# The order of one attention body: first scores before the router's transpose, the keys' projection before the fourth maxima product, the router's logits one place later

## The chip, the cores and the metric

One core of a Trainium2 chip runs the whole program. The metric is the device time in microseconds (us) of one execution. The kernel before was run three times: 950.31 us in the median, 949.5 the lowest and 953.55 the highest. The engines are TensorE (PE), VectorE (DVE), ScalarE (ACT), GpSimd (POOL) and SyncE (SP), which issues DMAs. Each runs its own list of instructions in order, and they meet at semaphores.

## The reference

Two layers work on x of shape (8, 256, 256). Each layer adds gated cross attention (16 heads of 16) and then a gated mixture of experts (8 experts, two per token) to x.

```python
x = x + tanh(g_xattn[0]) * attention(layernorm(x), ctx, L0 weights)
x = x + tanh(g_ffn[0])   * moe0(layernorm(x))      # logits = xn @ gate_w, top 2, softmax of the two, gelu experts
x = x + tanh(g_xattn[1]) * attention(layernorm(x), ctx, L1 weights)
x = x + tanh(g_ffn[1])   * moe1(layernorm(x))      # logits = xn @ router_w.T + b, softmax, top 2, capacity 256, relu experts
# attention: q, k, v = projections with bias; softmax(q k^T / 4) v per head; output projection with bias
```

The change is within the attention, in both layers. The attention phase also computes the router's layer norm and logits for the mixture that follows it.

## The kernel before, in words

`attention_phase` is called once for each layer. It works batch by batch (8 batches of 256 tokens) as a software pipeline written out by hand: each engine has a loop over "bodies" b = -3 to 9, and one body holds pieces of up to five batches. For the batch b+3 it makes the normalised input and turns it; for b+2 it projects queries, keys and values; for b+1 it takes the row maxima of the scores; for b it computes scores, exponentials and the weighted values; for b-1 it finishes the second half of the heads, the output projection and the residual; for b-2 it turns the router's rows and multiplies them with the gate's weights. Bodies 2 to 5 hold all of these (bodies 0 and 1 have no router work, bodies 6 to 9 have no projections of queries, keys and values any more). The order of the instructions in each engine is the order of the calls in its loop: TensorE L719 to L789, ScalarE L402 to L427, VectorE L529 to L565.

The pieces that the change touches, with their names in the code:

- `head_scores(b, i)`, i = 0 to 7 (L638): two products of 32 rows with 512 columns each, into the two banks `ps_max`. VectorE's `take_maxima(b, i)` (L463) reduces them (two reductions), and `head_scores(b, i+1)` waits until that is done, since the banks are used again.
- `scores(b, c)`, c = 0 to 3 (L658): 16 products of 17 rows (16 of the head and one with the row's maximum) into `ps_st`, the one buffer of four banks. `scores(b, 0)` waits for the DMAs that lay queries, keys and maxima into their slots; each of the four waits for the exponential before it, which frees `ps_st`. ScalarE's `probabilities(b, c)` (L386) is that exponential over 128x2048 elements.
- `weigh_values(b, c)` (L672): 16 products of the probabilities with the values, into `ps_head`; `turn_heads` (L685) turns the heads after ScalarE has copied them out (`heads`, L392), and VectorE's `normalise` (L473) divides by the sums.
- The bank `ps_lin` is a single buffer that eight pieces use in turn. In a full body of the kernel before, the turns are: queries, the router's transpose, the router's logits, keys, values, the transpose of the attention's output, the transpose of the normalised input, and the output projection. Each writes only after the one before it has been copied out by ScalarE or VectorE. ScalarE's `router_inputs` (L370) copies the router's transpose (semaphore `rt_ready`); VectorE's `router_logits` (L500) copies the logits (`lg_done`); ScalarE's `keys` copies the projected keys and adds their bias (`k_evac`); ScalarE's `separate_keys` (L347) then makes two masked copies of the keys for a later body's `head_scores`.

For batches whose keys are projected in the same body as a router turn (keys of batch 4 to 7, bodies 2 to 5), the projection waits for that body's router logits to have been copied:

```python
            def keys(b):
                pe.wait_ge(ctx_split, b + 1)
                wait(pe, lg_done, b - 3)
```

`fill` issues dummy transposes, only in bodies below 0 and above 6, where TensorE has less to do.

SP issues the DMAs of a body in a fixed order (L239 to L248): queries to slots, keys to slots, the context of batch b+4, the maxima of batch b+1 to slots, and the router's rows. The change leaves SP's and POOL's lists as they are.

Of the kernel before, what the change touches and what calls it, by code (L numbers as in the profile page):

```python
# [13 lines left out]
B, S, D = 8, 256, 256  # L14
# [68 lines left out]
def attention_phase(nc, layer, shared, dram, load_x):  # L83
# [4 lines left out]
    with ExitStack() as ctx:  # L88
# [249 lines left out]
        @block.scalar  # L338
        def _(act):
            def project(b, ps_sem, evac, ld, bias, compact):  # L340
                act.wait_ge(ps_sem, b + 1)
                wait(act, ld[(b - 2) % 3], SLOTTED * ((b - 2) // 3 + 1))
                for c in range(KC):
                    act.activation(compact[b % 2][:, c, :], ps_lin[:, c * S:(c + 1) * S], ACT.Identity,
                                   bias=bias[:, c:c + 1]).then_inc(evac, 1)

            def separate_keys(b):  # L347
                act.wait_ge(k_evac, 2 * b + 2)
                wait(act, s_ps, 8 * (b - 1))
                for j in range(2):  # L350
                    act.activation(k_r[b % 2][:, :, j, :], k_c[b % 2][:, :, :], ACT.Copy,
                                   scale=shared["odd_head"][:, j:j + 1]).then_inc(k_round, 1)

            def queries(b):
                wait(act, q_round, b - 1)
                if b == 0:
                    act.wait_ge(wq_ld, 32)
                project(b, q_ps, q_evac, q_ld, bq, q_c)

            def keys(b):  # L360
                if b == 0:
                    act.wait_ge(wk_ld, 32)
                project(b, k_ps, k_evac, k_ld, bk, k_c)

            def inputs(b):
                act.wait_ge(xt_ps, b + 1)
                wait(act, q_ps, b)
                act.activation(xn_t[0][:, :, :], ps_lin[:, :].rearrange("p (k s) -> p k s", k=KC), ACT.Copy).then_inc(xt_hi, 1)

            def router_inputs(b):  # L370
                act.wait_ge(rt_ps, b + 1)
                wait(act, lg_ps, b)
                act.activation(xr_t[:, :, :], ps_lin[:, :].rearrange("p (k s) -> p k s", k=KC), ACT.Copy).then_inc(rt_ready, 1)

            def maxima(b):
                act.wait_ge(mt_ps, b + 1)
                wait(act, m_ld, 16 * CH * b)
                act.activation(m_t[:, :], ps_max[0][0:H, :, :].rearrange("p q s -> p (q s)")[:, 0:S], ACT.Copy,
                               scale=-1.0).then_inc(mt_ready, 1)

            def outputs(b):
                act.wait_ge(ot_ps, b + 1)
                wait(act, out_ps, b)
                act.activation(o_t[0][:, :, :], ps_lin[:, :].rearrange("p (k s) -> p k s", k=KC), ACT.Copy).then_inc(ot_hi, 1)

            def probabilities(b, c):  # L386
                n = b * CH + c
                act.wait_ge(st_ps, n + 1)
                wait(act, pv_ps, n - 1)
                act.activation(prob[n % 2][:, :, :, :], ps_st[:, :, :, :], ACT.Exp, scale=HD ** -0.5).then_inc(prob_ready, 1)  # L390

            def heads(b, u):  # L392
                n = b * OCT + u
                act.wait_ge(pv_ps, 2 * n + 2)
                wait(act, turned, n - 1)
                act.activation(head_t[n % 2][:, :, :], ps_head[:, :].rearrange("p (c s) -> p c s", c=2), ACT.Copy).then_inc(head_out, 1)

            for n, w, ld in (("wq", wq, wq_ld), ("wk", wk, wk_ld), ("wv", wv, wv_ld), ("wo", wo, wo_ld)):
                act.wait_ge(ld, 32)
                act.activation(w[0][:, :, :], w_raw[n][:, :, :], ACT.Copy).then_inc(w_hi, 1)  # L400

            for b in BODIES:  # L402
                if is_batch(b + 2):
                    queries(b + 2)
                if is_batch(b - 1):
                    heads(b - 1, 1)
                if is_batch(b - 2):
                    router_inputs(b - 2)
                if is_batch(b):
                    probabilities(b, 0)  # L410
                if is_batch(b + 2):
                    keys(b + 2)
                    separate_keys(b + 2)
                if is_batch(b):
                    probabilities(b, 1)
                if is_batch(b - 1):
                    outputs(b - 1)
                if is_batch(b):
                    heads(b, 0)
                if is_batch(b + 3):  # L420
                    inputs(b + 3)
                if is_batch(b):
                    probabilities(b, 2)
                if is_batch(b + 1):
                    maxima(b + 1)
                if is_batch(b):
                    probabilities(b, 3)  # L427

        @block.vector
        def _(dve):  # L430
# [98 lines left out]
            for b in BODIES:  # L529
                if is_batch(b + 3):  # L530
                    if not load_x:
                        combine(b + 3)
                    moments(b + 3)
                if b == -3:
                    weights_first()
                if is_batch(b + 1):
                    take_maxima(b + 1, 0)
                    take_maxima(b + 1, 1)
                    take_maxima(b + 1, 2)
                if is_batch(b - 2):  # L540
                    router_logits(b - 2)
                if is_batch(b + 1):
                    take_maxima(b + 1, 3)
                if is_batch(b - 1):
                    normalise(b - 1, 1)
                if is_batch(b + 1):
                    take_maxima(b + 1, 4)
                if is_batch(b + 2):
                    values(b + 2)
                if is_batch(b + 1):  # L550
                    take_maxima(b + 1, 5)
                if is_batch(b - 1):
                    outputs_low(b - 1)
                if is_batch(b + 1):
                    take_maxima(b + 1, 6)
                if is_batch(b + 3):
                    inputs_low(b + 3)
                if is_batch(b + 1):
                    take_maxima(b + 1, 7)
                if is_batch(b - 1):  # L560
                    residual(b - 1)
                    router_moments(b - 1)
                if is_batch(b):
                    normalise(b, 0)
# [3 lines left out]
        def _(pe):  # L568
# [21 lines left out]
            def router_logits(b):  # L590
                if b == 0:
                    pe.wait_ge(gate_ld, 16 + 16 * layer)
                wait(pe, rt_ready, b + 1)
                for q in range(QT):
                    for k in range(KC):
                        ins = pe.matmul(ps_lin[:, q * E:(q + 1) * E], xr_t[:, k, q * P:(q + 1) * P], gate_w[:, k, :],
# [26 lines left out]
            def keys(b):  # L623
                if b == 0:
                    pe.wait_ge(w_split, 2)
                pe.wait_ge(ctx_split, b + 1)
                wait(pe, lg_done, b - 3)
                if b < 4:
                    wait(pe, q_evac, 2 * (b + 1))
                heads_project(wk, ctx_t[b % 2], k_ps)  # L630

            def values(b):
                if b == 0:
                    pe.wait_ge(w_split, 3)
                wait(pe, k_evac, 2 * (b + 1))
                token_major(ctx_t[b % 2], wv, v_ps)

            def head_scores(b, i):  # L638
# [80 lines left out]
            for b in BODIES:  # L719
# [10 lines left out]
                    head_scores(b + 1, 1)  # L730
                if is_batch(b - 1):
                    weigh_values(b - 1, 3)
                if is_batch(b - 2):
                    router_turn(b - 2)
                if is_batch(b + 1):
                    fill(b, True, 6 if b == -1 else 0)
                    head_scores(b + 1, 2)
                if is_batch(b):
                    scores(b, 0)
                if is_batch(b - 2):  # L740
                    router_logits(b - 2)
                if is_batch(b - 1):
                    turn_heads(b - 1, 1)
                    fill(b, False, 8)
                if is_batch(b + 1):
                    fill(b, True, 6 if b == -1 else 0)
                    head_scores(b + 1, 3)
                if is_batch(b + 2):
                    keys(b + 2)
                    fill(b, True, 6 if b == -2 else 0)  # L750
                if is_batch(b + 1):
                    fill(b, True, 6 if b == -1 else 0)
                    head_scores(b + 1, 4)
                if is_batch(b):
                    fill(b, False, 8)
                    scores(b, 1)
                if is_batch(b + 2):
                    values(b + 2)
                if is_batch(b + 1):
                    fill(b, True, 6 if b == -1 else 0)  # L760
                    head_scores(b + 1, 5)
                if is_batch(b):
                    weigh_values(b, 0)
                if is_batch(b - 1):
                    o_transpose(b - 1)
                    fill(b, False, 8)
# [758 lines left out]
```

## Time and profile before

| what | value |
|---|---|
| median of three runs | 950.31 us |
| the profiled execution's own time | 947.15 us |
| its span on the core | 945.4 us |
| mean granted TensorE clock, as a share of full speed | 0.901 |
| PE busy | 788.8 us (83%) |
| DVE busy | 640.2 us (68%) |
| ACT busy | 450.0 us (48%) |
| POOL busy | 361.9 us (38%) |

The span comes from one profiled execution. A busy share is an average over phases with different limits: the attention of layer 0 runs from about 14 to 232 us, its experts from about 260 to 550, the attention of layer 1 from about 563 to 800, and its experts to the end. Matmul ends are modelled, so a matmul's row is best read by its start and the start of what follows it.

### The profile page before, as it was taken

The numbers are of one execution on the slowest core, as the hardware profiler recorded it, in microseconds if no ns is written. First come the engines' busy times: TensorE is split into PE (matmuls) and PEld (weight loads), VectorE is DVE, ScalarE is ACT, GpSimd is POOL, SyncE is SP. The second block draws the span as 40 slices with busy tenths as digits, with TensorE's granted clock in tenths as the row PEclk, the third lists the DMA queues.
The fourth block names the chain that finished last, engine by engine and source line by source line (L and its number), as shares of the span: only waits on it lengthen the run. The fifth ranks groups of instructions, "written<-read, shape, count | busy, mean of one in ns | idle before, by whom it ended". The sixth has DMA issues, their size and how long they took to land. (4 is left out here: it accounts for less than half of the span.)

```text
span 945.4 us, 17859 instructions
## 1 busy us (share of the span) xinstructions
PE 788.8 (83%) x7040; PEld 670.8 (71%) x7040; DVE 640.2 (68%) x1172; ACT 450.0 (48%) x648; POOL 361.9 (38%) x390
## 2 busy tenths in 40 slices
PE   5799999896359999999999837899999896329995
PEld 4666777564359999999999836666667555328995
DVE  3667777632758999999999434676677632768883
ACT  2256666542056666666665211364556552315541
POOL 8434552112153333333331088656432112331653
PEclk8979999999569999999999967797999889558998
DMA  5211111000366777667774043222211000545732
GB/s 170 65 37 39 50 49 38 24 24 23 140 203 230 245 241 249 238 235 237 240 246 160 34 135 87 59 72 56 55 47 36 24 24 13 191 155 203 222 81 34
DMA packets 49814, 111.39 MB, mean 118 GB/s; under 512 B 11970, under 2 KB 35011, under 8 KB 42051
## 3 DMA queue, kind: packets, MB, share of 16 engines
q0 software_dynamic: 13056, 65.30, 21.7%
q1 hardware_dynamic: 36674, 44.95, 15.3%
q8 instruction: 56, 0.92, 0.4%
q14 instruction: 28, 0.22, 0.1%
HBM read 87.08 MB, written 14.49 MB: 107 GB/s over the span
## 5 line engine op out<-in xcount | busy, mean ns | idle before, releaser
L471 DVE TENSOR_REDUCE mx_a<-ps_max_a 128x2 f32<-128x512 f32 x256 | 164.4, 684 | 65.2 <-PE ps_max_a L647 63.0
L390 ACT ACTIVATE prob_a<-ps_st_a 128x2048 f32<-128x2048 f32 x64 | 120.0, 1875 | 56.9 <-PE ps_st_a L668 56.9
L71 PE MATMUL ps_h_e<-xe_t_e,w_e 128*128 128x256 f32 x480 | 140.2, 292 | 8.2 <-DVE xe_t_e L1380 8.2
L73 PE MATMUL ps_h_e<-xe_t_e,w_e 128*128 128x256 f32 x480 | 137.3, 286 | 0.0
L72 PE MATMUL ps_h_e<-xe_t_e,w_e 128*128 128x256 f32 x480 | 137.1, 286 | 0.0
L71 PE MATMUL ps_y_e<-w_e,h_e 128*128 128x256 f32 x480 | 133.2, 277 | 0.0
L72 PE MATMUL ps_y_e<-w_e,h_e 128*128 128x256 f32 x480 | 133.0, 277 | 0.0
L73 PE MATMUL ps_y_e<-w_e,h_e 128*128 128x256 f32 x480 | 133.0, 277 | 0.0
L1310 ACT ACTIVATE hid_e<-ps_h_e,b_e 128x256 f32<-128x256 f32 x184 | 78.4, 490 | 94.4 <-PE ps_h_e L73 94.4
L864 POOL DMA_INDIRECT w_raw_w<-L_w,block_row x46 | 43.6, 947 | 164.8 <-DVE b_e L1352 81.1
L71 PEld LDWEIGHTS ps_h_e<-xe_t_e,w_e 128*128 128x128 f32 x480 | 94.8, 198 | 9.4 <-DVE xe_t_e L1380 9.4
L72 PEld LDWEIGHTS ps_h_e<-xe_t_e,w_e 128*128 128x128 f32 x480 | 94.3, 196 | 0.0
L73 PEld LDWEIGHTS ps_h_e<-xe_t_e,w_e 128*128 128x128 f32 x480 | 93.9, 196 | 0.0
L71 PEld LDWEIGHTS ps_y_e<-w_e,h_e 128*128 128x128 f32 x480 | 90.3, 188 | 0.0
L73 PEld LDWEIGHTS ps_y_e<-w_e,h_e 128*128 128x128 f32 x480 | 90.2, 188 | 0.0
L72 PEld LDWEIGHTS ps_y_e<-w_e,h_e 128*128 128x128 f32 x480 | 90.2, 188 | 0.0
L647 PE MATMUL ps_max_a<-k_r_a,q_r_a 32*128 32x512 f32 x256 | 70.4, 545 | 20.9 <-DVE mx_a L471 18.8
L1361 DVE TENSOR_TENSOR h_e<-hid_e,h_e 128x512 fp32r<-128x512 f32 x120 | 83.1, 692 | 4.1
L280 POOL TENSOR_SCALAR r_var_eps_a<-r_mean_var_a 128x2 f32<-128x2 f32 x16 | 3.7, 229 | 213.4 <-DVE r_mean_var_a L498 213.4
L668 PE MATMUL ps_st_a<-q_s_a,k_s_a 17*128 17x256 f32 x1024 | 85.2, 415 | 0.0
L1292 ACT ACTIVATE w_e<-w_raw_w 128x1024 fp32r<-128x1024 f32 x60 | 64.7, 1082 | 33.2 <-PEq L59 33.2
L1336 DVE TENSOR_TENSOR w_e<-w_raw_w,w_e 128x1024 fp32r<-128x1024 f32 x60 | 72.9, 1217 | 5.3 <-ACT w_e L1292 5.3
(211 smaller groups left out, 1758.8 us busy)
## 6 DMA issues: line engine op xcount, KB each, us to landing
w_raw_w<-L_w SPq DMA_DIRECT2D x14, 1024.0 KB, 6.4
expert_out<-y_e SPq DMA_DIRECT2D x23, 256.0 KB, 4.7
ctx_raw_a<-ctx_t SPq DMA_DIRECT2D x16, 256.0 KB, 3.0
q_s_a<-q_c_a SPq DMA_DIRECT2D x128, 32.0 KB, 2.0
k_s_a<-k_c_a SPq DMA_DIRECT2D x128, 32.0 KB, 2.0
normalised<-xr SPq DMA_DIRECT2D x8, 256.0 KB, 2.2
normalised_weighted<-xr SPq DMA_DIRECT2D x8, 256.0 KB, 2.3
out<-x_sb SPq DMA_DIRECT2D x4, 512.0 KB, 3.0
```

Source lines behind the costliest of these rows:

```text
L71: pe.matmul(out, lhs[0], rhs[0], start=start, stop=False)
L72: pe.matmul(out, lhs[1], rhs[0], start=False, stop=False)
L73: return pe.matmul(out, lhs[0], rhs[1], start=False, stop=stop)
L390: act.activation(prob[n % 2][:, :, :, :], ps_st[:, :, :, :], ACT.Exp, scale=HD ** -0.5).then_inc(prob_ready, 1)
L471: dve.tensor_reduce(mx[:, q, h + 2 * j:h + 2 * j + 2], ps_max[j][:, :, :], AX.X, ALU.max).then_inc(max_done, 1)
L647: ins = pe.matmul(ps_max[j][:, :, :], q_r[b % 2][r:r + 32, c, q * P:(q + 1) * P], k_r[b % 2][r:r + 32, c, :, :], start=True, stop=True)
L668: ins = pe.matmul(ps_st[:, g, kt, :], k_s[b % 3][rows, c, kt * P:(kt + 1) * P], q_s[b % 3][rows, c, :], start=True, stop=True)
L864: pool.indirect_dma_start(out=buffers[which + "_raw"][b % 2][:, :], out_offset=None, in_=dram[which], in_offset=bass.IndirectOffsetOnAxis( ...
L1292: act.activation(w1[b % 2][0][:, k, :, :], w1_raw[b % 2][:, k * F:(k + 1) * F].rearrange("p (j f) -> p j f", j=FC), ACT.Copy).then_inc(w1_ ...
L1310: ins = act.activation(hid[jp % 2][:, j, :], ps_h[jp % RB][:, j, :], ACT.Gelu, bias=b1[b % 2][:, 2 * jp + j:2 * jp + j + 1])
L1336: ins = dve.tensor_tensor(w1[b % 2][1][:, k, :, :], w1_raw[b % 2][:, k * F:(k + 1) * F].rearrange("p (j f) -> p j f", j=FC), w1[b % 2][0][ ...
L1361: dve.tensor_tensor(h[b % 2][1][:, js, :], hid[jp % 2][:, :, :], h[b % 2][0][:, js, :].bitcast(F32), ALU.subtract).then_inc(h_ready, 1)
```

## The change

It is one of order, with the waits on `ps_lin` adapted to it. On TensorE, `scores(b, 0)` goes ahead of the router's transpose; `keys(b+2)` goes ahead of `head_scores(b+1, 3)` and follows `turn_heads(b-1, 1)` at once; the router's logits go from before `turn_heads` to behind `scores(b, 1)`; `weigh_values(b, 0)` goes ahead of `head_scores(b+1, 5)`. On ScalarE, the first exponential goes ahead of the copy of the router's transpose, and `separate_keys` goes behind the second exponential. On VectorE, the copy of the logits goes behind `take_maxima(b+1, 3)` and `normalise(b-1, 1)`. The turns of `ps_lin` become: queries, router's transpose, keys, router's logits, values, and the rest as before. So `keys` now waits for `rt_ready` (the copy of the router's transpose), the logits wait for the keys to have been copied out, and `values` waits for the logits.

```diff
# ScalarE's loop
                 if is_batch(b - 1):
                     heads(b - 1, 1)
+                if is_batch(b):
+                    probabilities(b, 0)
                 if is_batch(b - 2):
                     router_inputs(b - 2)
-                if is_batch(b):
-                    probabilities(b, 0)
                 if is_batch(b + 2):
                     keys(b + 2)
-                    separate_keys(b + 2)
                 if is_batch(b):
                     probabilities(b, 1)
+                if is_batch(b + 2):
+                    separate_keys(b + 2)
# VectorE's loop
                     take_maxima(b + 1, 2)
-                if is_batch(b - 2):
-                    router_logits(b - 2)
-                if is_batch(b + 1):
                     take_maxima(b + 1, 3)
                 if is_batch(b - 1):
                     normalise(b - 1, 1)
+                if is_batch(b - 2):
+                    router_logits(b - 2)
# TensorE's waits
             def router_logits(b):
-                wait(pe, rt_ready, b + 1)
+                if b < B - 4:
+                    wait(pe, k_evac, 2 * (b + 5))
+                if b >= B - 4:
+                    wait(pe, rt_ready, b + 1)
...
             def keys(b):
-                wait(pe, lg_done, b - 3)
+                wait(pe, rt_ready, b - 3)
...
             def values(b):
-                wait(pe, k_evac, 2 * (b + 1))
+                wait(pe, lg_done, b - 3)
+                if b < 4:
+                    wait(pe, k_evac, 2 * (b + 1))
# TensorE's loop
                     weigh_values(b - 1, 3)
+                if is_batch(b):
+                    scores(b, 0)
                 if is_batch(b - 2):
                     router_turn(b - 2)
                 if is_batch(b + 1):
                     head_scores(b + 1, 2)
-                if is_batch(b):
-                    scores(b, 0)
-                if is_batch(b - 2):
-                    router_logits(b - 2)
                 if is_batch(b - 1):
                     turn_heads(b - 1, 1)
-                if is_batch(b + 1):
-                    head_scores(b + 1, 3)
                 if is_batch(b + 2):
                     keys(b + 2)
                 if is_batch(b + 1):
-                    head_scores(b + 1, 4)
+                    head_scores(b + 1, 3)
                 if is_batch(b):
                     scores(b, 1)
+                if is_batch(b - 2):
+                    router_logits(b - 2)
+                if is_batch(b + 1):
+                    head_scores(b + 1, 4)
                 if is_batch(b + 2):
                     values(b + 2)
+                if is_batch(b):
+                    weigh_values(b, 0)
                 if is_batch(b + 1):
                     head_scores(b + 1, 5)
-                if is_batch(b):
-                    weigh_values(b, 0)
```

## Rows read from the trace of the kernel before

**Rows 1.** Busy time by stretch, layer 0, bodies 3 and 6.
```profile
core 0: us, PE busy (x) PEld busy (x) DVE busy (x) ACT busy (x) POOL busy (x), PEclk, DMA share, GB/s
...
110.56:132.31 21.75, 21.41 (x231) 15.22 (x224) 16.14 (x34) 13.71 (x16) 10.40 (x12) 1.00 0.19 51
...
175.25:197.10 21.85, 18.90 (x186) 11.43 (x182) 13.81 (x28) 10.27 (x9) 3.38 (x4) 0.84 0.05 15
```

**Rows 2.** The same view, bodies 2 to 4 of layer 1.
```profile
645.61:674.04 28.43, 26.10 (x231) 18.66 (x224) 18.20 (x38) 13.76 (x16) 14.35 (x16) 0.82 0.18 47
674.04:699.20 25.16, 22.84 (x230) 15.82 (x224) 17.98 (x38) 13.77 (x16) 10.42 (x12) 0.93 0.17 44
699.20:722.93 23.73, 21.39 (x231) 15.20 (x224) 18.10 (x38) 13.72 (x16) 10.43 (x12) 1.00 0.14 36
```

**Rows 3.** Timeline of PE in body 3 of layer 0: start, us, instruction, [idle before].
```profile
114.26 1.07 PE L681 MATMUL ps_head_a<-prob_a,v_a 128*32 128x256 f32 x16
115.26 0.66 PE L572 MATMUL ps_lin_a<-ident,xr 128*128 128x128 f32 x4
115.84 0.50 PE L647 MATMUL ps_max_a<-k_r_a,q_r_a 32*128 32x512 f32 x2
115.94 1.27 PE L668 MATMUL ps_st_a<-q_s_a,k_s_a 17*128 17x256 f32 x16
117.14 1.06 PE L596 MATMUL ps_lin_a<-gate_w_a,xr_t_a 128*128 128x8 f32 x8
118.06 0.63 PE L690 MATMUL ps_head_a<-ident,head_t_a 128*128 128x128 f32 x4
118.62 0.50 PE L647 MATMUL ps_max_a<-k_r_a,q_r_a 32*128 32x512 f32 x2
119.05 0.39 PE L71 MATMUL ps_lin_a<-ctx_t_hi_a,wk_hi_a 128*128 128x256 f32 x1
...
120.67 1.36 PE L668 MATMUL ps_st_a<-q_s_a,k_s_a 17*128 17x256 f32 x16
...
125.00 0.66 PE L572 MATMUL ps_lin_a<-ident,o_a 128*128 128x128 f32 x4
```

**Rows 4.** Timeline of ACT in the same body.
```profile
115.39 0.60 ACT L396 ACTIVATE head_t_a<-ps_head_a 128x512 f32<-128x512 f32 x1 [1.71 <-PE ps_head_a L681]
115.95 0.60 ACT L373 ACTIVATE xr_t_a<-ps_lin_a 128x512 f32<-128x512 f32 x1
117.29 1.88 ACT L390 ACTIVATE prob_a<-ps_st_a 128x2048 f32<-128x2048 f32 x1 [0.74 <-PE ps_st_a L668]
```

**Rows 5.** Timeline of DVE in the same body.
```profile
118.24 0.17 DVE L509 COPY logits<-ps_lin_a 128x16 f32<-128x16 f32 x1 [0.56 <-PE ps_lin_a L596]
119.16 1.29 DVE L471 TENSOR_REDUCE mx_a<-ps_max_a 128x2 f32<-128x512 f32 x2 [0.75 <-PE ps_max_a L647]
...
120.65 0.42 DVE L481 TENSOR_TENSOR o_a<-ps_head_a,rsum_a 128x256 f32<-128x256 f32 x1
```

**Rows 6.** Timeline, layer 1's start: ACT copies keys; PE then begins the values.
```profile
571.91 0.84 ACT L344 ACTIVATE k_c_a<-ps_lin_a,bk_a 128x256 f32<-128x256 f32 x2 [2.12 <-PE ps_lin_a L73]
...
572.89 0.36 PE L71 MATMUL ps_lin_a<-wv_hi_a,ctx_t_hi_a 128*128 128x256 f32 x1 [0.43 <-ACT k_c_a L344]
```

**Rows 7.** Timeline of SP: the maxima's four DMAs, issued for the body from 132.31.
```profile
132.03 2.20 SPq L207 DMA_DIRECT2D q_s_a<-m_t_a  x4
```

**Rows 8.** Timeline of PE, layer 0, bodies 6 and 7.
```profile
184.71 0.79 PE L647 MATMUL ps_max_a<-k_r_a,q_r_a 32*128 32x512 f32 x2 [1.38 <-DVE mx_a L471]
...
198.42 2.29 PE L681 MATMUL ps_head_a<-prob_a,v_a 128*32 128x256 f32 x32 [0.78 <-DVE o_a L481]
201.47 0.66 PE L572 MATMUL ps_lin_a<-ident,xr 128*128 128x128 f32 x4 [0.77 <-POOL xr L286]
202.06 1.15 PE L668 MATMUL ps_st_a<-q_s_a,k_s_a 17*128 17x256 f32 x16
203.14 1.06 PE L596 MATMUL ps_lin_a<-gate_w_a,xr_t_a 128*128 128x8 f32 x8
```

More of the change, by code:

```diff
@@ L744, in _ @@
                     fill(b, False, 8)
-                if is_batch(b + 1):
-                    fill(b, True, 6 if b == -1 else 0)
-                    head_scores(b + 1, 3)
                 if is_batch(b + 2):
@@ L756, in _ @@
                     scores(b, 1)
+                if is_batch(b - 2):
+                    router_logits(b - 2)
+                if is_batch(b + 1):
+                    fill(b, True, 6 if b == -1 else 0)
+                    head_scores(b + 1, 4)
                 if is_batch(b + 2):
                     values(b + 2)
+                if is_batch(b):
+                    weigh_values(b, 0)
                 if is_batch(b + 1):
```

## The prediction, written before the changed kernel ran

> **What bounds the kernel now.** I read the busy time by stretch first, cutting the attention at each body's first maxima product (`head_scores` 0). In layer 0 a full body takes 21.75 us and TensorE is busy for 21.41 of them, at a clock of 1.00 [rows 1]; DVE has 16.14 and ACT 13.71. So in the full bodies TensorE's list sets the time, at most 0.34 us of it idle, and whatever makes TensorE wait there lengthens the kernel nearly one for one. In layer 1 the bodies 2 to 4 take 28.43, 25.16 and 23.73 us with the same instructions; the clock column (0.82, 0.93, 1.00) is what differs [rows 2]. The experts, over half the span, aren't touched, and I charge them nothing.
>
> Then the timelines of one full body, PE, ACT and DVE side by side [rows 3 to 5]. I count from the body's start at 110.56. The reader is to see that PE's starts follow one another without a bracket of idle time, and that the exponential at 117.29 begins only when the scores before it end: ACT had nothing to do for 0.74 us there. That idle time is what moving the scores up addresses. It isn't on the path: PE doesn't wait for this exponential.
>
> **The change in a full body, step by step.** No instruction is added or removed; starts move. From the rows I take slots, that is start to next start on PE: weighing of values 1.00 (114.26 to 115.26), router's transpose 0.58, maxima product followed by a projection 0.43 (118.62 to 119.05), maxima product and scores together 1.30 (115.84 to 117.14), logits 0.92, heads' turn 0.56, a projection 1.62 (119.05 to 120.67) [rows 3]. Scores alone, with no maxima product beside them, are 1.08 (202.06 to 203.14) [rows 8].
>
> - Up to the end of the second weighing nothing changes, so PE is free at 115.26, which is 4.70 in the body. The first scores start there if their maxima have landed. SP issues these four DMAs over 2.20 us from 0.28 before the body starts [rows 7], so the last is issued before 1.92, and it has 2.8 us left to land. I don't charge this wait; if it bound, everything below would come later by as much.
> - Scores 4.70, router's transpose 5.78, maxima product 2 at 6.36, heads' turn 6.79. PE reaches the keys at 7.35.
> - The keys may not start before ACT has copied the router's transpose. ACT's list now has the exponential ahead of that copy. The scores end 1.15 after their start [rows 8], at 5.85; the exponential starts 0.08 later, as now (117.21 to 117.29), at 5.93, takes 1.88 and ends at 7.81; the copy takes 0.60 and ends at 8.43 with a gap of 0.02 [rows 4]. A projection starts 0.14 us after the ACT copy that frees the bank (572.75 to 572.89) [rows 6]. The keys start at 8.57: **PE stands for 1.22 us**. Before, the copy was done at 5.99 and nobody waited. Queued behind the waiting keys are all of PE's later pieces, the third maxima product and the second scores first, although their inputs are there.
> - Before, the keys started at 8.49 (119.05), so at the same place in the body. But by then PE had done the logits and maxima product 3 too. Both now come later, and here the price appears: keys 8.57, maxima product 3 with scores 1 at 10.19, logits 11.48 (the keys are copied out by 11.1), maxima product 4 at 12.40, PE free for the values at 12.83.
> - The values now wait for DVE's copy of the logits, which stands behind the reduction 3 and the normalisation. Reduction 3 starts some 0.6 after its product and takes 1.29, to 12.07; the normalisation ends 0.62 after the reduction (120.45 to 121.07), at 12.69; the copy takes 0.17, to 12.86 [rows 5]; with the 0.14 as above the values start at 13.00, a **second wait of 0.17**.
> - Values 13.00, weighing 14.62, maxima product 5 at 15.62, output's transpose 16.05. It started at 14.44 before (125.00). The body is 1.61 us late here. Reduction 5 and with it the low part of the output come behind maxima product 5, which now has the weighing ahead of it; this adds 0.12 before the input's transpose. The rest of the body keeps its order and its waits, so it shifts as a whole.
>
> The sum for a full body: 1.61 + 0.12 = 1.73, from 21.75 to 23.5. The slack of 0.34 could take at most that much off: 1.4 to 1.75. In layer 1 the bodies 2 to 4 first have a wait of some 2 us for the combining of the experts' rows, before the second maxima product; it shifts all of what is above alike and covers none of it. Four full bodies a layer, two layers: **8 x 1.73 = +13.8 us**.
>
> **The other bodies.** Bodies 0 and 1 have no router. Their scores fill a short wait for reduction 1, and the fourth maxima product then waits longer for its reduction; DVE's chain of eight reductions sets them. I take +0.2 each, +0.8 in all, with -1 to +1 each as ends. In body 7 TensorE waits for POOL's router rows: the weighing ends its slots at 200.38, the transpose starts at 201.47 [rows 8]. The scores (1.08) now lie in that gap of 1.09: -1.08, and no keys are there to wait. In body 6 the wait of 0.36 for the same rows is filled, and later TensorE again waits for reductions (1.38 at 184.71 [rows 8]); following the chain gives -0.8. In body 8 the logits' wait for ACT's copy is filled by the heads' turn and the dummies: -0.3. Together -2.2 a layer, **-4.4 us**. The separation of the keys comes 1.9 us later on ACT, but its result is read a body later, and ACT is idle for some 8 us of 21.75 [rows 1]: nothing. SP's queue is passed by no DMA.
>
> So far +10.2 us. **The clock** is the term that rows don't price exactly. At 1.2 GHz (half of 2.4) matmuls take twice as long. Body 2 of layer 1 against body 4, same instructions, is 4.7 us longer, body 3 1.4 [rows 2]; both had a PE wait of 2 us before the clock fell, but body 4 had the same wait and no fall. Body 6 (0.84) fell behind the wait of 1.38 us [rows 1, 8]. The change adds a wait of 1.22 us to eight bodies; the falls in bodies 6 may go. The ends are -8 (the two falls of rows 2 and those of bodies 6 gone) and +25 (eight more of the mean price of 3.05). I take one fall more than now, +3, nearest to layer 0's full bodies, which have none. The sum is +13.2. On the profiled execution's own 947.15 us that gives 960.3; the median shown is 3.2 us above it, and I put the sum on the median: **963.5 us**.
>
> The Trainium skill (TensorE: Matmul & The Clock Gate, "A second HAM failure mode: psum-queue depth-cycling") says that frequent short idles between groups of matmuls can make the clock swing between its two levels. The trace agrees in layer 1, where one of three like bodies stayed at 1.00, and disagrees in layer 0's bodies, whose waits are short. What it gives is rival A.
>
> **Rivals.**
> A. The clock falls in steady bodies that are at 1.00 now. For it: the new wait stands among products that use 17 or 32 of the array's rows, in each full body, and body 6 fell behind 1.38 us. Against: body 4 of layer 1 bore 2 us. With four more falls at 3.05 beyond mine: 975.7 us.
> B. Not slower: the exponentials, not PE's list, set the bodies. `ps_st` is a single buffer, the first exponential comes 0.68 us earlier, and if the later three followed it, each full body would be 0.68 shorter: 8 x -0.68 - 4.4 = -9.8, 940.5 us. It decides only if the keys start by 7.4 in the body. Against it: scores 1 stand behind the keys in PE's list, and the keys behind ACT's copy.
> C. TensorE's waits land where layer 1 or the last bodies had them anyway, and falls of the clock go: half of the 13.8, the tail's -4.4, no clock term, -4 for falls in bodies 6: 950.3 + 6.9 + 0.8 - 4.4 - 4 = 949.6 us. It needs slack that rows 1 don't show.
> D. The change doesn't do what it says, because the DMAs of the maxima hold the first scores back until their old place. Then scores start at 5.38, the keys at 9.25, the full body is 0.68 longer still: 8 x 0.68 = +5.4, 968.9 us.
>
> **How the numbers follow.** My case has 0.60, A 0.15, D 0.07, B 0.08, C 0.10. My case's own range is 957 to 971, from 1.4 us a full body and no clock term up to two more falls. With A's part up to four falls and short of B and C: 954 to 975.5. What this measurement can tell from no change is 0.5%, 4.75 us: 945.6 to 955.1. Slower: my case, A and D, 0.82 less a little for its lower end: 0.80. Same: C and such a lower end, 0.11. Faster: B and a clock better than mine, 0.09.
>
> **What would show it right or wrong.** In a full body of the changed kernel the first row of the keys (L71, ctx_t) should carry an idle bracket of about 1.2 us put down to ACT's xr_t, and the first row of the values one of 0.1 to 0.3 from DVE's logits; neither has one now. Bodies 3 and 4 of layer 0 should take 23.2 to 23.7 us with PE's busy time near 21.4. In body 7 the wait for POOL's xr should be gone. If the keys start without a wait, or the full bodies stay near 21.75, the central step is wrong; if the bodies lengthen as said but the whole differs by over 5 us, it is the clock.

## The result, and the profile after

Over 20 runs each, taken side by side, the kernel before takes 948.73 us in the median and the changed one 956.19 us. The ratio is 1.0077, with a 95% interval of 1.0053 to 1.0101: slower by about 7.3 us, where +13.2 was forecast (a ratio of 1.014). The sign and the place are as forecast, and 956.19 lies in the outer range of 954 to 975.5, though just under the 957 that the main case had as its lower end; the size is little more than half of the forecast one. One of the 20 runs of the changed kernel and four of the experiments' were in a slower state of the chip, and the ratios leave them out.

The changed kernel's profiled execution has a span of 949.5 us at a mean clock of 0.906, against 945.4 us before; at 951.26 us it was one of the kernel's faster runs. First bodies 3 to 8 of layer 0, in the view of busy time by stretch (us; PE, PEld, DVE, ACT, POOL busy; granted clock; DMA share; GB/s). The stretches run from one residual update of DVE to the next, which is a body's length too.

```profile
111.88:134.92 23.04, 21.74 (x224) 15.24 (x223) 16.10 (x34) 13.64 (x16) 10.40 (x12) 1.00 0.18 48
134.92:157.97 23.05, 21.76 (x224) 15.24 (x223) 16.10 (x33) 13.65 (x16) 10.39 (x12) 1.00 0.15 37
157.97:180.52 22.55, 21.05 (x220) 14.75 (x219) 14.53 (x29) 13.04 (x15) 3.94 (x5) 1.00 0.15 36
180.52:201.83 21.31, 19.43 (x184) 11.43 (x183) 13.93 (x27) 10.16 (x9) 3.38 (x4) 0.84 0.05 15
201.83:219.69 17.86, 16.93 (x200) 12.36 (x199) 3.87 (x12) 9.85 (x9) 3.38 (x4) 1.00 0.09 31
219.69:232.28 12.59, 10.52 (x108) 7.98 (x106) 3.86 (x11) 4.00 (x5) 3.38 (x4) 1.00 0.07 22
```

Body 3 takes 23.04 us, where it took 21.75 [rows 1]: +1.29, at the same clock of 1.00. Idle time of PE goes from 0.34 to 1.30, and its busy time rises by 0.33 with the same instructions; part of that is that maxima product 2 and the first scores took 1.30 us side by side [rows 3] and now take 1.07 and 0.43 one behind the other. Bodies 6, 7 and 8 of layer 0, cut in the same way, took 22.02, 18.74 and 13.07 before; they are 0.71, 0.88 and 0.48 shorter. Body 6 is at a clock of 0.84 before and after.

Now PE in body 3, which starts at 113.21 (start, us, instruction, idle before). It answers to [rows 3].

```profile
116.90 1.07 PE L686 MATMUL ps_head_a<-prob_a,v_a 128*32 128x256 f32 x16
117.90 1.15 PE L673 MATMUL ps_st_a<-q_s_a,k_s_a 17*128 17x256 f32 x16
118.97 0.66 PE L572 MATMUL ps_lin_a<-ident,xr 128*128 128x128 f32 x4
119.56 0.50 PE L652 MATMUL ps_max_a<-k_r_a,q_r_a 32*128 32x512 f32 x2
119.99 0.66 PE L695 MATMUL ps_head_a<-ident,head_t_a 128*128 128x128 f32 x4
121.62 0.36 PE L71 MATMUL ps_lin_a<-ctx_t_hi_a,wk_hi_a 128*128 128x256 f32 x1 [0.97 <-ACT xr_t_a L373]
...
123.24 1.34 PE L673 MATMUL ps_st_a<-q_s_a,k_s_a 17*128 17x256 f32 x16
124.51 1.06 PE L599 MATMUL ps_lin_a<-gate_w_a,xr_t_a 128*128 128x8 f32 x8
125.50 0.50 PE L652 MATMUL ps_max_a<-k_r_a,q_r_a 32*128 32x512 f32 x2
125.93 0.39 PE L71 MATMUL ps_lin_a<-wv_hi_a,ctx_t_hi_a 128*128 128x256 f32 x1
...
128.97 0.66 PE L572 MATMUL ps_lin_a<-ident,o_a 128*128 128x128 f32 x4
```

The scores start where the router's transpose did, and the keys carry the forecast bracket: 0.97 us, put down to ACT's copy. The keys start 8.41 us into the body (8.49 before), with the logits and a maxima product still to come. The output's transpose is at 15.76, where it was at 14.44.

ACT in the same body, answering to [rows 4]:

```profile
119.11 1.88 ACT L390 ACTIVATE prob_a<-ps_st_a 128x2048 f32<-128x2048 f32 x1 [0.48 <-PE ps_st_a L673]
120.89 0.59 ACT L373 ACTIVATE xr_t_a<-ps_lin_a 128x512 f32<-128x512 f32 x1
```

The copy begins as the exponential ends. PE's waits from 28 to 235 us (total us, times, longest):

```profile
PE ps_max_a L652 <- DVE mx_a L472: 4.4, 8, 0.8
PE ps_lin_a L71 <- ACT xr_t_a L373: 3.9, 4, 1.0
...
PE ps_st_a L673 <- DMA q_s_a<-m_t_a: 0.3, 1, 0.3
```

The wait on the copy stands four times in layer 0, once for each full body. The maxima's DMA was waited for once (0.3 us, body 0). The wait of body 7 for POOL's router rows (0.77 [rows 8]) is gone.

Layer 1's bodies 2 to 4 took 28.43, 25.16 and 23.73 us [rows 2]; after:

```profile
649.70:676.28 26.58, 23.26 (x224) 16.28 (x223) 18.12 (x38) 13.65 (x16) 14.37 (x16) 0.94 0.19 51
676.28:704.78 28.50, 26.18 (x224) 18.03 (x223) 18.04 (x38) 13.65 (x16) 10.41 (x12) 0.82 0.15 39
704.78:729.83 25.05, 21.72 (x224) 15.20 (x223) 18.04 (x37) 13.64 (x16) 10.44 (x12) 1.00 0.14 34
```

At a clock of 1.00 the loss is 25.05 - 23.73 = 1.32 again; where the clock falls it lengthens a body by 1.5 to 3.5 us here and by 1.4 to 4.7 us before. Body 6 of layer 1 took 22.94 us at 0.78 before and takes 18.83 at 1.00 now. From run to run the time goes with the clock: 19 runs of the changed kernel lie between 947.6 and 961.4 us at mean clocks of 0.910 to 0.891, with a correlation of -0.96.

The two profiles differ by 4.1 us: the eight full bodies are 9.3 us longer, bodies 6 to 8 are 7.5 shorter (4.1 of it body 6 of layer 1), bodies up to 1 of layer 0 are 1.4 longer, and the experts with the start of layer 1 are 0.9 longer. The medians differ by some 7, so some 3 us stand in no profile that was kept.

### The profile page after: what moved, and what is told of

The parts are those of the page before. It is cut to its first block and busy times, and to the rows that moved or that the text cites. A ratio compares the mean times of both kernels' runs of the same rounds, so it can differ in the third digit from the quotient of the medians.

```text
span 949.5 us, 17859 instructions
## 1 busy us (share of the span) xinstructions
PE 789.8 (83%) x7040; PEld 670.4 (71%) x7040; DVE 639.9 (67%) x1172; ACT 449.0 (47%) x648; POOL 362.0 (38%) x390
## 5 line engine op out<-in xcount | busy, mean ns | idle before, releaser
L673 PE MATMUL ps_st_a<-q_s_a,k_s_a 17*128 17x256 f32 x1024 | 82.0, 415 | 0.3 <-DMA q_s_a<-m_t_a 0.3
```

Of the source, the lines that this page charges most:

```text
L673: ins = pe.matmul(ps_st[:, g, kt, :], k_s[b % 3][rows, c, kt * P:(kt + 1) * P], q_s[b % 3][rows, c, :], start=True, stop=True)
```

## Experiments

Ratios are to the kernel before, timed on the same chip. Where bodies of a run are compared, there is one profile of it.

**1. ScalarE's copy ahead of the exponential again**, all else changed.

```diff
+                if is_batch(b - 2):
+                    router_inputs(b - 2)
                 if is_batch(b):
                     probabilities(b, 0)
-                if is_batch(b - 2):
-                    router_inputs(b - 2)
```

> The changed kernel with one part undone: ScalarE copies the router's transpose ahead of the first exponential again; TensorE's order stays changed. Theory (the new wait of the keys on ScalarE's copy, which stands behind a 1.88 us exponential, is most of the loss): TensorE waits 0.97 us at the keys in each full body of the changed kernel; here the copy ends some 7.1 us into the body and the keys start at 7.35 without a wait. The exponential starts at 7.1 and ends at 8.95, when the second scores are due, so a full body takes 22.0 to 22.2 us (before 21.75, changed 23.04); over eight full bodies +2.8, with the -4 of bodies 6 to 8: 0.998 of the kernel before, 0.990 of the changed one. Rival (the logits moved behind the second scores, and the chain logits-copy-values, are the loss): the full body stays at 22.8 to 23.1 and the kernel at 1.006 or more. Rival (the exponentials' chain is what counts): the full body gets longer than 23.04, since the first exponential is 1.2 us later.

Measured: 1.0034 (1.001 to 1.0059). Layer 0's bodies 4 and 5:

```profile
130.24:152.09 21.85, 21.52 (x224) 15.28 (x223) 16.11 (x34) 13.65 (x16) 10.41 (x12) 1.00 0.16 39
152.09:174.97 22.88, 22.36 (x220) 15.64 (x219) 14.53 (x28) 13.04 (x15) 3.94 (x5) 0.93 0.14 36
```

The full body is 21.85 us, 1.19 under the changed kernel's: the copy's place behind the exponential is the loss in the body, and all the rest of the change costs 0.10. Both rivals fall. But the whole missed its forecast of 0.998: it is only 0.4% better than the changed kernel, not the 1.0% of 8 x 1.19 us. Body 5 fell to 0.93 here, and in layer 1 body 0 took 22.96 us at 0.70 and body 1 23.82 at 0.93, where the kernel before had 21.68 at 0.76 and 20.23 at 1.00.

That start of layer 1 shows how far one profile can be trusted on the clock. From layer 1's first reduction to the end of body 1 no router work runs, and the changed kernel and experiments 1, 4, 6, 8 and 12 have the same instructions there in the same order; they took 59.4, 65.0, 64.1, 58.0, 58.1 and 64.6 us, at clocks of 0.89, 0.84, 0.84, 0.91, 0.94 and 0.79.

**2. Late logits only**: experiment 1, and the first scores behind maxima product 2 again.

```diff
-                if is_batch(b):
-                    scores(b, 0)
                 if is_batch(b - 2):
                     router_turn(b - 2)
                 if is_batch(b + 1):
                     head_scores(b + 1, 2)
+                if is_batch(b):
+                    scores(b, 0)
```

> The changed kernel with the first scores behind the third maxima product again and ScalarE's copy ahead of the exponential again: what is left of the change is the keys' earlier place, the later logits and the order of the weighing. Theory: no wait at the keys (they start 7.15 into the body), scores and maxima product share 1.30 us again; a full body takes 21.8 to 21.9 us, +0.1; bodies 6 and 7 lose the gain that they had from the scores in POOL's wait; in all 1.000 of the kernel before. Rival (late logits are the loss): full body 22.5 or more, 1.006.

Measured: 1.0095 (1.0059 to 1.013), a miss. Bodies 2 to 4 of layer 0:

```profile
89.30:112.47 23.17, 22.84 (x224) 16.21 (x223) 16.10 (x33) 13.72 (x16) 10.39 (x12) 0.93 0.15 36
112.47:134.10 21.63, 21.30 (x224) 15.29 (x223) 16.12 (x33) 13.72 (x16) 10.43 (x12) 1.00 0.19 51
134.10:157.28 23.18, 22.86 (x224) 16.54 (x223) 16.11 (x33) 13.71 (x16) 10.39 (x12) 0.93 0.15 36
```

At full clock the body is shorter than before (21.63 against 21.75), so the late logits cost nothing by themselves. But in two of the three bodies the clock fell. The timeline of PE around the first fall, at 102 us:

```profile
99.22 0.50 PE L652 MATMUL ps_max_a<-k_r_a,q_r_a 32*128 32x512 f32 x2
99.30 1.28 PE L673 MATMUL ps_st_a<-q_s_a,k_s_a 17*128 17x256 f32 x16
100.52 1.06 PE L599 MATMUL ps_lin_a<-gate_w_a,xr_t_a 128*128 128x8 f32 x8
101.50 0.50 PE L652 MATMUL ps_max_a<-k_r_a,q_r_a 32*128 32x512 f32 x2
101.94 0.39 PE L71 MATMUL ps_lin_a<-wv_hi_a,ctx_t_hi_a 128*128 128x256 f32 x1
...
102.28 0.28 PE L73 MATMUL ps_lin_a<-wv_lo_a,ctx_t_hi_a 128*128 128x256 f32 x1
...
102.74 0.42 PE L73 MATMUL ps_lin_a<-wv_lo_a,ctx_t_hi_a 128*128 128x256 f32 x1
```

The products of the values' projection go from 0.28 to 0.42 us: the granted clock is 1.00 up to 102.5 and 0.50 behind it. No idle bracket stands in the ten us ahead. The engine was busy, in the last of them with products of 32 or 17 rows or of 8 columns, one behind the other. The other fall of this layer (146.9 us), two in experiment 6 (101.5 and 125.4) and the one in experiment 1 (165.4) come at the same place, 1.5 to 2.1 us after the start of the 8-column products and without idle time ahead. The stretch doesn't bring a fall each time: layer 0's full bodies of the changed kernel have it too, at 123.24 to 125.93 above for one, and stayed at 1.00; in layer 1 one of them fell behind it (at 666 us). Experiments 7 to 9 test the stretch.

These falls are not the whole loss of this profile. Its span is 10.0 us over the one before; the eight full bodies are 2.3 of that, and bodies up to 1 of both layers, which have no router's product, 7.2.

**3. First scores and exponential early only**, logits and keys as before.

```diff
# in the kernel before: TensorE
+                if is_batch(b):
+                    scores(b, 0)
                 if is_batch(b - 2):
                     router_turn(b - 2)
...
-                if is_batch(b):
-                    scores(b, 0)
                 if is_batch(b - 2):
                     router_logits(b - 2)
# and probabilities(b, 0) ahead of router_inputs(b - 2) on ScalarE
```

> The kernel before with the other part alone: first scores ahead of the router's transpose, and the first exponential ahead of ScalarE's copy; logits, keys and values in their old places. Theory: the logits' product now is what waits for the copy, from 6.8 to 8.2 us in the body, with the heads' turn, maxima product 3 and the keys queued behind it; a full body takes 23.3 to 23.5 us (+1.6), the last bodies gain some 3 to 4 us in all; 1.010 of the kernel before. Rival (earlier scores pay and the loss is from the later logits): full body 21.1 to 21.7, 0.99 of the kernel before.

Measured: 1.0548 (1.0505 to 1.0591), a miss: the sign and the place are right, the loss is five times the forecast one. PE in body 3 of layer 0:

```profile
124.42 1.26 PE L596 MATMUL ps_lin_a<-gate_w_a,xr_t_a 128*128 128x8 f32 x8 [1.47 <-ACT xr_t_a L373]
125.53 1.09 PE L690 MATMUL ps_head_a<-ident,head_t_a 128*128 128x128 f32 x4
126.56 0.79 PE L647 MATMUL ps_max_a<-k_r_a,q_r_a 32*128 32x512 f32 x2
```

The wait of 1.47 us now stands right ahead of the 8-column products, and the clock falls behind it (the turn of the heads takes 1.09 instead of 0.63). All eight full bodies had a fall; bodies 2 to 4 of layer 1 took 30.5 us each at 0.78. Half of the change is thus far worse than all of it. In the changed kernel the wait is shorter (0.97) and stands ahead of the keys' projection; experiment 4 bears on which of the two matters.

**4. The suspected wait made longer**: ScalarE copies the router's transpose twice.

```diff
+                act.activation(xr_spare[b % 2][:, :, :], ps_lin[:, :].rearrange("p (k s) -> p k s", k=KC), ACT.Copy)
                 act.activation(xr_t[:, :, :], ps_lin[:, :].rearrange("p (k s) -> p k s", k=KC), ACT.Copy).then_inc(rt_ready, 1)
```

> The changed kernel in which ScalarE copies the router's transpose twice (first into a spare buffer that nobody reads), so that the suspected wait is 0.6 us longer. Theory: the wait of the keys goes from 0.97 to 1.55 us and a full body from 23.04 to 23.6 us; eight bodies make +4.7 us, 1.005 of the changed kernel, 1.013 of the one before, plus what the clock does: if waits of this length make the granted clock fall, some full bodies of layer 0 show it below 1.00 and the whole loses more. Rival (the wait is covered elsewhere in the body): 23.04 to 23.1 stays.

Measured: 1.0161 (1.0132 to 1.0189), and PE's waits in layer 0's full bodies:

```profile
PE ps_lin_a L71 <- ACT xr_t_a L375: 5.9, 4, 1.5
```

The single wait is 1.46 in place of 0.97 and the body 23.53 in place of 23.04 at full clock: the wait goes through to the body one for one. Eight times 0.49 is 4 us of the some 8 us by which it is slower than the changed kernel; bodies 2 and 5 of layer 0 are at 0.93 and layer 1's 2 to 4 at 0.73 to 0.82, so the rest goes with the clock. Against experiment 3 the wait is as long (1.46 and 1.47), but ahead of the keys' projection and not of the 8-column products, and the loss is 1.6% and not 5.5%: what follows the wait makes more of a difference than its length from 0.97 to 1.46. The orders differ in more than that, and the wide product was not tried in experiment 3.

**5. The changed order in bodies 6 to 9 only.** On all three engines the calls that the change moves stand twice, with conditions on b:

```diff
+                if is_batch(b) and b >= 6:
+                    scores(b, 0)
                 if is_batch(b - 2):
                     router_turn(b - 2)
...
-                if is_batch(b):
+                if is_batch(b) and b < 6:
                     scores(b, 0)
```

> The changed order in bodies 6 to 9 alone; bodies up to 5 keep the order of the kernel before. Theory (the change gains where TensorE waits for POOL's router rows and no keys are projected, and loses in the full bodies): bodies 6, 7 and 8 get shorter by 0.7, 0.9 and 0.5 us as in the changed kernel's trace, full bodies stay at 21.75; both layers -4.1 us, 0.9957 of the kernel before. Rival (the last bodies' gain in one profile was the clock's doing): 1.000.

Measured: 0.9975 (0.9949 to 1.0002). Bodies 7 and 8 take 17.85 and 12.64 us in both layers, as in the changed kernel, at a clock of 1.00 (18.74 and 13.07 before), and the full bodies 21.7. The gain of bodies 7 and 8, 2.7 us over both layers, is the order's, not the clock's. Body 6 took 21.35 us at 0.92 and 22.49 at 0.85, where it took 22.02 at 0.84 and 22.94 at 0.78, so what the order alone is worth there isn't told apart from the clock. The whole gained some 2.4 us of the forecast 4.1, with an interval that reaches no gain.

**6. The router's copy on VectorE**, the exponential still first on ScalarE.

```diff
# VectorE, behind take_maxima(b + 1, 1)
+                if is_batch(b - 2):
+                    router_inputs(b - 2)     # dve.tensor_copy(xr_t, ps_lin)
```

> The changed kernel with the copy of the router's transpose moved from ScalarE to VectorE, behind the second pair of reductions; the exponential stays first on ScalarE. Theory (it is the place of the copy behind the exponential, not the early exponential, that costs): the wait at the keys is gone and a full body takes 21.8 to 22.0 us, like the kernel with the copy first on ScalarE (21.85), although the first exponential is 1.1 us earlier than there. Rival (early exponentials pay once the keys don't wait): full body under 21.6. Whole: about 1.000 to 1.004 of the kernel before, as the one with the copy first (1.0034).

Measured: 0.9986 (0.9953 to 1.0018). The wait at the keys is gone; a full body without a fall takes 21.97 us. The early exponential brings nothing (21.85 with it late), and takes next to nothing as long as nobody's copy stands behind it. Two of layer 0's full bodies fell to 0.93.

**7 to 9. Width of the router's product.** The gate's 8 columns are read eight times over, 64 columns, and 8 of the results are used; the number of instructions stays.

```diff
-                        ins = pe.matmul(ps_lin[:, q * E:(q + 1) * E], xr_t[:, k, q * P:(q + 1) * P], gate_w[:, k, :],
+                        ins = pe.matmul(ps_lin[:, q * 8 * E:(q + 1) * 8 * E], xr_t[:, k, q * P:(q + 1) * P], spread(gate_w[:, k, :], 1, 8),
```

7, in the late-logits kernel of experiment 2:

> The kernel with the late logits only, with the router's product made eight times as wide (the gate's 8 columns repeated to 64, of which 8 are read; same number of instructions). Late logits only had a full body of 21.63 us at full clock, under the 21.75 of before, and yet 1.0095 in time: in layer 0's bodies 2 and 4 the granted clock fell although TensorE wasn't idle, behind maxima product, scores, logits and maxima product in a row, which use 32 or 17 rows or 8 columns. Theory (the clock falls behind such a stretch of thin products): with wider products in the middle of it the falls in layer 0's full bodies go, and the kernel is at 0.995 to 1.002 of the one before. Rival (falls come by chance or by idle time only): bodies still fall to 0.93, ratio 1.007 to 1.012. Cost of the width itself: the product's slot goes from 0.98 to at most 1.2 us.

8, in the changed kernel:

> The changed kernel with the same wide router's product. If the changed kernel's loss is the waits in its full bodies alone (8 x 1.29 us less 4.1), this stays at 1.006 to 1.008 of the kernel before. If falls of the clock behind the thin products are a part of it, it comes to 1.000 to 1.004.

9, in the kernel before:

> The kernel before with the router's product 64 columns wide, nothing else. It prices the width by itself. In the kernel before the product stands between the first scores and the heads' turn (wide transposes), and layer 0's full bodies didn't fall; so theory: 0.996 to 1.001, less than the 0.9 per cent that the width gave to the late logits (1.0095 to 1.0003). Rival (width helps every order alike): 0.990 to 0.994.

Measured: 1.0003 (0.9967 to 1.004), 1.0019 (0.9992 to 1.0046) and 0.9985 (0.996 to 1.0011). So the width alone took 0.9% off the late logits, 0.6% off the changed kernel, and nothing that can be told off the kernel before, where the product stands ahead of wide transposes. The mean granted clock of the runs says the same: its median went from 0.893 (experiment 2) to 0.903, from 0.899 (changed kernel) to 0.907, and stayed at 0.901 for the kernel before. Bodies 2 and 4 of layer 0 in 7, which had been at 0.93:

```profile
87.13:108.81 21.68, 21.34 (x224) 15.30 (x223) 16.16 (x34) 13.71 (x16) 10.40 (x12) 1.00 0.16 39
...
130.48:152.20 21.72, 21.39 (x224) 15.34 (x223) 16.16 (x33) 13.72 (x16) 10.41 (x12) 1.00 0.16 39
```

In 8 the full bodies still take 23.1 us at full clock: the width leaves the waits alone. This tells two costs apart that the changed kernel has together, the waits and the falls behind the narrow product. Which bodies of the changed kernel gained by the width no profile shows: the one kept of it is of a faster run and has one such fall. The start of layer 1 isn't cured; it took 64.2 us at 0.81 in 7.

**10. Both cures in the kernel before**: the last bodies' order and the wide product.

> The kernel before with the changed order in bodies 6 to 9 and the router's product 64 columns wide. Theory: -4.1 us from the last bodies, and fewer falls of the clock behind the thin products (body 6 of both layers fell in most profiles): 0.988 to 0.995 of the kernel before. If width only helps where the logits stand late, 0.996, as the tail alone (0.9975).

Measured: 0.997 (0.9936 to 1.0004). The width adds nothing that can be told to 0.9975 here; body 6 still fell to 0.85 in both layers. The second branch of the expectation fits better.

**11. Late wide logits, first scores early in bodies 6 to 9 only** (experiment 7 with the last bodies of the change).

> Late logits, wide, without the scores' early place in bodies up to 5 and with it in bodies 6 to 9. Full bodies as in the wide late-logits kernel (21.7 us, none fallen in layer 0), last bodies as in the changed kernel (17.85 and 12.6 us for bodies 7 and 8, where the wide late logits had 18.89 and 12.69): 1.0003 less 0.2 per cent, 0.996 to 0.999 of the kernel before.

Measured: 936.59 us, **0.9894** (0.9862 to 0.9926). It beats both kernels and is better than its forecast, which is a miss too. Bodies 5 to 7 of layer 0:

```profile
152.06:173.26 21.20, 20.68 (x220) 14.86 (x219) 14.59 (x29) 13.12 (x15) 3.94 (x5) 1.00 0.16 39
173.26:192.13 18.87, 16.47 (x184) 10.30 (x183) 13.88 (x28) 10.16 (x9) 3.38 (x4) 1.00 0.05 17
192.13:210.03 17.90, 16.97 (x200) 12.35 (x199) 3.86 (x11) 9.84 (x9) 3.38 (x4) 1.00 0.09 31
```

Body 6 takes 18.87 us at 1.00 (18.88 in layer 1), where it took 22.02 and 22.94; I had not counted that its fall of the clock would go. That is 7.2 of the 11.0 us between this profile and the one before.

**12. The changed kernel with the copy first in bodies up to 5, and the wide product.**

> The changed kernel with ScalarE's copy ahead of the exponential in bodies up to 5 (no wait at the keys) and the wide product. Against the changed kernel with the wide product alone (1.0019) it takes away 8 x 1.2 us of waiting: 0.990 to 0.993 of the kernel before if the waits in the full bodies were a loss in full. Rival (without the waits the clock falls more, as it did in the copy-first kernel, which lost only 0.4 per cent less than the changed one): 0.997 to 1.002.

Measured: 0.9899 (0.9851 to 0.9946), from five runs. Against 1.0019 of experiment 8, 1.2% is gone with the wait; 8 x 1.2 us is 1.0%. With the thin stretch widened the waits are worth about what they measure in the body. In its profile layer 0's full bodies are all at 1.00, though layer 1's 2 to 4 are at 0.87. That profile is the slowest of the five runs.

## Why the prediction was off in size

- **What bounds a full body** was right: TensorE's list. In the changed kernel (0.97 us of wait, +1.29 us of body) and with the longer copy (+0.49, +0.49) PE's waits appear in the body; nothing absorbed them. The rival that needed slack falls, by experiment 4. PE's busy time was forecast to stay near 21.4 and rose to 21.74, though the slots of the sum had the scores and the maxima product apart.
- **The wait of the keys on the copy behind the exponential** was right in place, with 0.97 for 1.22. The step that failed in size is the chain from the exponential to the input's transpose, which gave a full body +1.73 and measured +1.29 (bodies 3 and 4 were to take 23.2 to 23.7 us and took 23.04 and 23.05). I let each instruction on ACT and DVE start at the end that the profile gives for the one ahead, or 0.02 later. No row shows that gap of 0.02: in [rows 4] the router's copy starts 0.04 before the printed end of the one ahead, and in [rows 5] the reciprocal 0.09 before the reduction's. Here the copy starts at 120.89, 0.10 before the exponential's printed end (119.11 + 1.88), and so the keys start at 8.41, not 8.57. On DVE the reciprocal of the normalisation and the logits' copy started 0.08 and 0.06 before such ends. The other 0.09 of the difference in the wait is only how it is counted: the bracket runs from the heads' turn's printed end, 0.66 us after its start, my sum from its slot of 0.56.
- **The second wait**, 0.17 at the values, isn't there: they start at 12.72 instead of 13.00, when both their slot and the logits' copy are due. This chain too was built from printed ends. Keys and values together make 0.29 of the 0.44 by which the body was put too long: the output's transpose comes 1.32 late, not 1.61.
- **The 0.12 for the output's low part** was an error: in the changed kernel ScalarE's copy of the output is done 0.1 us before the reduction ahead of the low part, so the two come together. The input's transpose is at 17.92 where I had 18.33. The full body is +1.29 for +1.73 forecast: 8 x 0.44 = 3.5 us of the error.
- **Bodies 6 to 8**: -2.07 us in layer 0 for -2.2. Experiment 5 shows bodies 7 and 8 (0.9 and 0.4 a layer) at full clock; body 6's share of the order alone isn't shown. It was worth more where its fall of the clock went with it: in layer 1 the changed kernel's bodies 6 to 8 are 5.4 us shorter, 4.1 of it body 6 (22.94 to 18.83).
- **The clock**: I took +3 us for it and +0.8 for bodies 0 and 1. Waits and last bodies, with the last bodies of layer 0 for both layers, make 8 x 1.29 - 4.1 = +6.2 of the 7.3 measured, so bodies 0 and 1 and the clock together are some +1 for +3.8, and the measured change is known to some 2.3 us either way. The figure was within its ends, but the reason was incomplete: I tied falls to idle time alone. It is a balance of falls that come and falls that go, as in body 6 of layer 1. Experiment 2 had no new wait and lost 0.95%; the width of a product undid it, and the same width took 5.5 us off the changed kernel, so falls behind the narrow product were part of its time.
- **Rivals.** A (falls in steady bodies) didn't come in layer 0 of the changed kernel's profile but did in experiments 1, 2, 3, 4 and 6; the rule that I cited for it from the Trainium skill (TensorE: Matmul & The Clock Gate, "A second HAM failure mode: psum-queue depth-cycling"), of short idles, doesn't cover the falls of experiment 2, ahead of which there was no idle; the measurement decides. B (exponentials) falls by experiments 1 and 6. C has no slack to stand on. D showed up once, 0.3 us in body 0.

The error of 5.9 us is thus 3.5 from the full body's chain, and the rest is the term for the clock with bodies 0 and 1, as a remainder. Layer 1's full bodies go on falling with the wide product (0.87 in 2 to 4 in experiment 12, one fall in experiment 11). Those falls begin at another place, within 2 us after the wait of 2.0 us for the maxima that each of these bodies has (experiment 12: the waits end at 655.07, 682.03 and 709.03, the clock falls at 656.3, 683.6 and 710.9). Not settled: why some bodies bear that wait and others don't.

## What to carry to other kernels

Where one bank is handed on from piece to piece, find the copy that frees it and look at what stands ahead of it on its engine: an instruction of 1.88 us put ahead of a copy of 0.60 delays everything behind the bank, though the long one gets its inputs earlier. When you add up a chain on one engine, take the distance from start to start from rows, not printed ends. And judge an order at full clock and by its falls apart: a reorder that shortens the body by 0.12 us lost 0.95%, and widening eight products that nobody needed wider brought it back. One profile doesn't price a fall of the clock: the same instructions took 58 to 65 us in six of them. An order that pays only where an engine waits anyway can be applied to those bodies alone.

## What the runs showed of the hardware

TensorE's granted clock fell from 1.00 to 0.50 (2.4 to 1.2 GHz) without idle time ahead of it: at 102 us of experiment 2 the engine had been issuing without a gap for over 10 us, at last through products with 32 and 17 rows and with 8 columns. Five falls of layer 0 in experiments 1, 2 and 6 came at this place, and none did in layer 0's full bodies of the six kernels with the wide product. Making the 8-column products 64 columns wide cost almost nothing (the eight took 1.10 instead of 1.06 us, and the next instruction came 1.03 instead of 0.98 us after they began) and the two falls in layer 0's full bodies were gone. In full bodies of the same order a fall to a mean of 0.93 cost 1.4 to 1.6 us (25.16 against 23.73, 23.17 against 21.63) and one to 0.82 cost 3.5 to 4.7 (28.50 against 25.05, 28.43 against 23.73). Back-to-back instructions on ScalarE and VectorE can start before the printed end of the one ahead, by 0.06 to 0.10 us in the rows used here.
